# One signal per group, part or half; VectorE's row sum in a PSUM bank; row numbers in eight compare-and-multiply passes

## The reference, cut to what matters

```
# block 1 (cut): projection, 4-tap convolution, SiLU, chunked scan, gate, RMS norm, projection
zxbcdt = u @ W_in;  z, xBC, dt = split(zxbcdt)
xBC = silu(conv_b + sum_i pad(xBC)[i:i+s] * conv_w[i]);  x, B, C = split(xBC)
y = ssd(x * dt, -exp(A_log) * dt, B, C) + x * D
x1 = layernorm(u + rms(y * silu(z)) * norm_scale @ W_out)
# block 2: product-key retrieval, 8 heads, 8 rows each
h   = silu(x1 @ W_up.T + b_up) @ W_down.T + b_down
q   = h @ W_q.T                                    # two halves, 8 heads, 64 wide
sim = q . keys                                     # 64 keys in each half
scores, idx = top_k(sim, 8)                        # per half and head
all_scores  = sx[:, None] + sy[None, :]            # 64 pairs
all_indices = ix[:, None] * 64 + iy[None, :]
sc, pk  = top_k(all_scores, 8)
indices = take(all_indices, pk)                    # 64 row numbers per token
z   = silu((h . down_embed[indices]) * softmax(sc))
out = layernorm(x1 + sum_k z[k] * up_embed[indices[k]])
```

## Time and profile before

| | us |
|---|---|
| median of the runs (lowest, highest) | 3226.48 (3216.73, 3239.93) |
| the profiled execution, its own time | 3229.48 |
| its span, first to last instruction | 3227.5 |
| busy: TensorE, VectorE, ScalarE, GpSimd | 2906.3, 2840.0, 1672.4, 2251.4 |
| granted TensorE clock, mean | 0.959 |
| a gather, median from issue to landing | 4.7 |

### The profile page before, as it was taken

How to read it: one execution, slowest core, us unless ns; L and a number is a source line. 1 busy time by engine, 2 the same in 40 slices (tenths; PEclk the granted TensorE clock), 3 DMA queues, 4 the chain that set the end, 5 groups by cost and what they waited for, 6 DMA issues and landing times.

```text
span 3227.5 us, 50404 instructions
## 1 busy us (share of the span) xinstructions
PE 2906.3 (90%) x13856; PEld 1939.0 (60%) x13856; DVE 2840.0 (88%) x10664; ACT 1672.4 (52%) x4833; POOL 2251.4 (70%) x2056
## 2 busy tenths in 40 slices
PE   8899999999998999999998999999999999999864
PEld 8665566665556666556666655666665566665441
DVE  0579999899999999999999999999999999999986
ACT  0546554555555555555555565555555554555521
POOL 0047777777777777777777777777777777777776
PEclk9999999999999999999999999999999999999976
DMA  5258888888888888888888888888888888888887
GB/s 189 111 176 276 272 267 275 283 271 276 273 262 270 287 276 273 275 278 257 284 287 274 269 278 277 266 284 282 274 273 273 274 265 283 281 271 273 270 287 252
DMA packets 189354, 857.11 MB, mean 266 GB/s; under 512 B 36176, under 2 KB 39376, under 8 KB 188048
## 3 DMA queue, kind: packets, MB, share of 16 engines
q0 software_dynamic: 163840, 805.44, 76.2%
q1 hardware_dynamic: 19104, 34.87, 3.2%
q10 hardware_dynamic: 6128, 13.60, 1.1%
HBM read 845.38 MB, written 8.39 MB: 265 GB/s over the span
## 4 chain that ended last, share of the span: by engine, by line
DVE 41%; PE 29%; issue 10%; DMA 10%; ACT 7%; POOL 2%; DVEq 0%; POOLq 0%; ACTq 0%; SPq 0%
DVE acc L1053 11%; DVE ring L1034 10%; DMA ring<-embed,idx 9%; PE bank L457 9%; PE bank L416 7%; PE bank L307 4%; DVE xc L866 3%; PE bank L445 3%; POOL ring L262 2%; DVE i L953 2%; PE bank L290 2%; DVE v L946 1%; ACT L587 1%; ACT L676 1%; DVE zp L1040 1%
## 5 line engine op out<-in xcount | busy, mean ns | idle before, releaser
L262 POOL DMA_INDIRECT ring<-embed,idx x2048 | 2250.1, 1099 | 961.5 <-issue 494.6
L1034 DVE SCALAR_TENSOR_TENSOR ring<-ring,hcur 128x256 f32<-128x256 f32 x2048 | 831.2, 421 | 145.7 <-DMA ring<-embed,idx 141.0
L1053 DVE SCALAR_TENSOR_TENSOR acc<-ring,coef,acc 128x512 f32<-128x512 f32 x1248 | 935.3, 749 | 11.1 <-ACT coef L587 10.9
L457 PE MATMUL bank<-ring,diag_c 128*128 128x512 f32 x1536 | 812.9, 652 | 136.4 <-ACT diag_c L583 136.4
L583 ACT ACTIVATE diag_c<-cst,zp 128x128 f32<-128x128 f32 x768 | 278.6, 399 | 909.4 <-DVE zp L1040 877.7
L457 PEld LDWEIGHTS bank<-ring,diag_c 128*128 128x128 f32 x1536 | 289.8, 205 | 451.1 <-ACT diag_c L583 256.4
L416 PEld LDWEIGHTS bank<-zs,w_up 128*128 128x128 f32 x4096 | 470.8, 192 | 51.3 <-issue 31.2
L416 PE MATMUL bank<-zs,w_up 128*128 128x128 f32 x4096 | 476.4, 276 | 0.8 <-ACT zs L685 0.8
L307 PEld LDWEIGHTS bank<-ut,w_in 128*128 128x128 f32 x2560 | 293.6, 193 | 15.4 <-issue 15.4
L307 PE MATMUL bank<-ut,w_in 128*128 128x128 f32 x2560 | 293.9, 277 | 0.5 <-issue 0.5
L587 ACT ACTIVATE coef<-zp 128x3 f32<-128x3 f32 (+3 forms) x576 | 113.7, 197 | 333.9 <-DVE zp L1040 333.5
(11 more groups left out here) (132 smaller groups left out, 3544.8 us busy)
## 6 DMA issues: line engine op xcount, KB each, us to landing
ring<-embed,idx POOLq DMA_INDIRECT x2048, 4.7
ring<-uT SPq DMA_DIRECT2D x4, 2048.0 KB, 10.1
ut<-uT SPq DMA_DIRECT2D x32, 256.0 KB, 6.6
zs<-u SPq DMA_DIRECT2D x32, 256.0 KB, 5.7
out<-acc SPq DMA_DIRECT2D x32, 256.0 KB, 5.5
w_in<-W_in ACTq DMA_DIRECT2D x1, 4608.0 KB, 21.1
w_up<-W_upT ACTq DMA_DIRECT2D x1, 4096.0 KB, 19.1
w_out<-W_out ACTq DMA_DIRECT2D x1, 2048.0 KB, 9.5
```

What stands on the lines that cost most here:

```text
L262: pool.indirect_dma_start(out=ring[:, k % RING, :], out_offset=None, in_=embed, in_offset=bass.IndirectOffsetOnAxis(ap=idx[:, half, k:k + ...
L457: pe.matmul(bank[SUM][:, :], diag_c[:, n % DIAGS, :], ring[:, k % RING, DP:ROW], start=(n == 0), stop=(n == len(PE_ROWS) - 1)).then_inc(ro ...
L1034: dve.scalar_tensor_tensor(out=ring[:, k % RING, 0:DP], in0=ring[:, k % RING, 0:DP], scalar=1.0, in1=hcur[:, :], op0=ALU.mult, op1=ALU.mul ...
L1053: dve.scalar_tensor_tensor(out=total, in0=ring[:, k % RING, DP:ROW], scalar=coef[:, k:k + 1], in1=x1[:, :] if n == 0 else total, op0=ALU.m ...
```

## The change

It does six things.

1. `running`, the sum of the D rows, lies in PSUM bank 3. The first `weigh` of a tile reads `x1` and writes `running`, the next 38 read and write it, the last writes `total` in SBUF. The wait for `o_ok` moves from the first to the last.
2. The other stages share six banks instead of seven, so most of them move, with other waits. The third and the fourth step sum wait for the first and the second gate; `turn_x` begins after the first exponential; `z_proj` waits for the last convolution input; the up projections for `new_state`'s halves.
3. `row_pe` is signalled once per group, after its last P row; the gathers and ScalarE's buffers wait for the group. `DIAGS` is 4.
4. One signal per part of the convolution, per quarter of `up_silu`, per group of dots, for both halves of `y_off` and of `y_diag`.
5. Row numbers: mask and shift into one tensor `place`; then eight passes of 128 elements, each `(place == n) * i1[n]`, written with a stride of eight into `hot`; one reduction of 1024 elements.
6. The fence increments go, on VectorE, GpSimd and SyncE.

```diff
-DIAGS = 3
+DIAGS = 4
+PE_GRPS = [g for g in range(NGRP) if "P" in GROUPS[g]]
+NPG = len(PE_GRPS)
+def signal_of(k):
+    return PE_GRPS.index(max(g for g in PE_GRPS if FIRST[g] <= k)) + 1
...
-        hot = xdt[:, BANK:DI].rearrange("p (k c) -> p k c", k=PICKS)
+        hot = xdt[:, :].rearrange("p (g k a) -> p g k a", g=NG, a=TOP)
...
-        Z_BANKS, SEG_BANKS, XT_BANKS, MISC, YOFF_BANKS = (0, 2), (4, 1, 3, 0), (1, 3), 2, (4, 0)
-        Y_BANKS, ST_BANKS, YT_BANKS, OP, XBC_BANKS = (6, 7), (1, 3), (2, 4), 0, (6, 7, 1)
-        X1T, UP_BANKS, DOWN, HT, SIM_BANKS, SUM = 3, (2, 4, 0, 6), 7, 1, (6, 7), 5
+        Z_BANKS, SEG_BANKS, XT_BANKS, MISC, YOFF_BANKS = (0, 2), (4, 1, 0, 2), (4, 1), 0, (2, 0)
+        Y_BANKS, ST_BANKS, YT_BANKS, OP, XBC_BANKS = (6, 7), (4, 1), (2, 0), 6, (7, 2, 0)
+        X1T, UP_BANKS, DOWN, HT, SIM_BANKS, SUM = 6, (4, 1, 7, 2), 6, 6, (7, 6), 5
+        running = bank[3]
...
             def gathers(t, half, first):
                 pool.wait_ge(idx_ok, t + 1)
-                pool.sem_inc(pool_fence, 1)
...
-                            pool.wait_ge(row_pe, len(PE_ROWS) * of + PE_ROWS.index(j) + 1)
+                            pool.wait_ge(row_pe, NPG * of + signal_of(j))
...
-                        pool.sem_inc(pool_fence, 1)
...
             def step_sums(i, b):
-                if b == 0:
-                    pe.wait_ge(tap_ok, KC * (i + 1))
-                if b == 3:
-                    pe.wait_ge(z_ok, 2 * i + 1)
+                if b >= 2:
+                    pe.wait_ge(z_ok, 2 * i + b - 1)
...
-                    pe.matmul(bank[SUM][:, :], diag_c[:, n % DIAGS, :], ring[:, k % RING, DP:ROW],
-                              start=(n == 0), stop=(n == len(PE_ROWS) - 1)).then_inc(row_pe, 1)
+                    m = pe.matmul(bank[SUM][:, :], diag_c[:, n % DIAGS, :], ring[:, k % RING, DP:ROW],
+                                  start=(n == 0), stop=(n == len(PE_ROWS) - 1))
+                if rows_of(g, "P"):
+                    m.then_inc(row_pe, 1)
...
             def places(i):
                 dve.wait_ge(top2_ok, 4 * i + 2)
-                dve.tensor_scalar(bk[:, :], pk_v, TOP - 1, None, ALU.bitwise_and).then_inc(top2_ok, 1)
+                dve.tensor_scalar(place[:, 1, :, :], pk[:, :, :], TOP - 1, None, ALU.bitwise_and).then_inc(top2_ok, 1)
...
+                for n in range(TOP):
+                    dve.scalar_tensor_tensor(out=hot[:, :, :, n], in0=place[:, :, :, :].rearrange("p b n k -> p (b n) k"),
+                                             scalar=float(n), in1=i1[:, :, n:n + 1].to_broadcast([P, NG, TOP]),
+                                             op0=ALU.is_equal, op1=ALU.mult).then_inc(pick_ok, 1)
 
             def numbers(i):
+                dve.wait_ge(pick_ok, TOP * (i + 1))
+                dve.tensor_reduce(ixy[:, :, :], hot.rearrange("p (b n) k a -> p b (n k) a", b=2), AX.X, ALU.add).then_inc(ixy_ok, 1)
...
                 n = DVE_ROWS.index(k)
                 if n == 0:
                     dve.wait_ge(saved_ok, t + 1)
-                    if not first:
-                        dve.wait_ge(o_ok, t)
-                else:
+                if n > 0 or not first:
                     dve.wait_ge(row_used, len(DVE_ROWS) * t + n)
-                dve.scalar_tensor_tensor(out=total, in0=ring[:, k % RING, DP:ROW], scalar=coef[:, k:k + 1],
-                                         in1=x1[:, :] if n == 0 else total,
+                if n == len(DVE_ROWS) - 1 and not first:
+                    dve.wait_ge(o_ok, t)
+                dve.scalar_tensor_tensor(out=total if n == len(DVE_ROWS) - 1 else running[:, :],
+                                         in0=ring[:, k % RING, DP:ROW], scalar=coef[:, k:k + 1],
+                                         in1=x1[:, :] if n == 0 else running[:, :],
                                          op0=ALU.mult, op1=ALU.add).then_inc(row_used, 1)
```

More of the change, by code:

```diff
@@ L120, in build @@
         v2 = sb("v2", [P, EH, TOP])
-        pk = sb("pk", [P, EH, TOP], U32)
-        bk = sb("bk", [P, PICKS], U32)
-        ixy = sb("ixy", [P, 2, PICKS])
+        place = sb("place", [P, 2, EH, TOP], U32)
+        pk = place[:, 0, :, :]
         idx = sb("idx", [P, 2, PICKS], U32)
@@ L303, in xbc_proj @@
                         pe.wait_ge(y_ok, 2 * i)
-                        pe.wait_ge(st_ok, 2 * i - 1)
+                if part == 1 and not first:
+                    pe.wait_ge(yT_ok, 2 * i)
                 for c in range(4 * part, min(4 * part + 4, KC)):
@@ L350, in y_off @@
                 for b in range(2):
-                    pe.matmul(bank[YOFF_BANKS[b]][:, :], xc[:, KX + 1, :], state[:, b * BANK:(b + 1) * BANK],
-                              start=True, stop=True).then_inc(yoff_mm, 1)
+                    if b == 1:
+                        pe.wait_ge(dec_ok, 4 * i + 4)
+                    m = pe.matmul(bank[YOFF_BANKS[b]][:, :], xc[:, KX + 1, :], state[:, b * BANK:(b + 1) * BANK],
+                                  start=True, stop=True)
+                m.then_inc(yoff_mm, 1)
             def y_diag(i, first, b):
@@ L411, in up_proj @@
                     pe.wait_ge(x1T_ok, i + 1)
-                if b == 3 and ahead:
-                    pe.wait_ge(tap_ok, KC * (i + 1) + 4)
+                if b < 2:
+                    pe.wait_ge(st_ok, 2 * i + b + 1)
+                elif ahead:
+                    pe.wait_ge(tap_ok, PARTS * (i + 1) + b - 1)
                 for c in range(4 * b, 4 * b + 4):
@@ L434, in turn_h @@
                 pe.wait_ge(h_ok, i + 1)
-                if ahead:
-                    pe.wait_ge(tap_ok, KC * (i + 2))
                 for c in range(KP):
@@ L857, in time_steps, with convolve @@
                                          op0=ALU.mult, op1=ALU.mult).then_inc(cur_ok, 1)
-            def convolve(i, j, lo, hi):
-                for c in range(lo, hi):
-                    if j == 0:
-                        dve.wait_ge(tap_ok, KC * i + c + 1)
-                    else:
-                        dve.wait_ge(conv_ok, KC * (3 * i + j - 1) + c + 1)
-                    dve.scalar_tensor_tensor(out=xc[:, c, :], in0=raw[:, c, j:j + P], scalar=taps[:, c, j:j + 1],
-                                             in1=xc[:, c, :], op0=ALU.mult, op1=ALU.add).then_inc(conv_ok, 1)
+            def convolve(i, j, part):
+                if j == 0:
+                    dve.wait_ge(tap_ok, PARTS * i + part + 1)
+                else:
+                    dve.wait_ge(conv_ok, PARTS * (3 * i + j - 1) + part + 1)
+                for c in range(4 * part, min(4 * part + 4, KC)):
+                    m = dve.scalar_tensor_tensor(out=xc[:, c, :], in0=raw[:, c, j:j + P], scalar=taps[:, c, j:j + 1],
+                                                 in1=xc[:, c, :], op0=ALU.mult, op1=ALU.add)
+                m.then_inc(conv_ok, 1)
             def scaled_x(i):
@@ L992, in places @@
                 dve.wait_ge(top2_ok, 4 * i + 3)
[L993 to L999 removed]
+                dve.tensor_scalar(pk[:, :, :], pk[:, :, :], 3, None, ALU.logical_shift_right).then_inc(top2_ok, 1)
@@ L1029, in uses, with dot @@
                 return len(range(k % RING, PICKS, RING))
-            def dot(t, k):
+            def dot(t, k, last):
                 dve.wait_ge(row_in[k % RING], 16 * (uses(k) * t + k // RING + 1))
-                dve.scalar_tensor_tensor(out=ring[:, k % RING, 0:DP], in0=ring[:, k % RING, 0:DP], scalar=1.0,
-                                         in1=hcur[:, :], op0=ALU.mult, op1=ALU.mult,
-                                         accum_out=zp[:, k:k + 1]).then_inc(dot_ok, 1)
+                m = dve.scalar_tensor_tensor(out=ring[:, k % RING, 0:DP], in0=ring[:, k % RING, 0:DP], scalar=1.0,
+                                             in1=hcur[:, :], op0=ALU.mult, op1=ALU.mult,
+                                             accum_out=zp[:, k:k + 1])
+                if last:
+                    m.then_inc(dot_ok, 1)
             def times_prob(t, g):
-                dve.wait_ge(dot_ok, PICKS * t + FIRST[g + 1])
+                dve.wait_ge(dot_ok, NGRP * t + g + 1)
                 dve.tensor_tensor(zp[:, FIRST[g]:FIRST[g + 1]], zp[:, FIRST[g]:FIRST[g + 1]],
@@ L1074, in group @@
                     if n < len(mine):
-                        dot(t, mine[n])
+                        dot(t, mine[n], n == len(mine) - 1)
                     if n < len(late):
@@ L1184, in _ @@
             for j in range(TAPS - 1):
-                convolve(0, j, 0, KC)
+                for part in range(PARTS):
+                    convolve(0, j, part)
             dve.wait_ge(w_out_in, 16)
```

99 lines of the change are left out of this document (38 added, 61 removed).

## The result

The kernel after takes 3075.8 us (median of four runs, 3069.4 to 3081.0) against 3225.1 us for the kernel before beside it: ratio 0.9524, 95% interval 0.9498 to 0.955. The rival "All of it comes", 3079 us, is the case that came. The profiled execution has a span of 3070.2 us and a mean granted clock of 0.979 (before 0.959).

What follows compares the result with a forecast made beforehand. Bound: a loop through GpSimd's gathers, VectorE and TensorE, 94.8 us a tile. Terms -2.6 and -0.3 gave 91.9, taken as 92.3 beside floors 90.5 and 91.3; -2.5 us x 32 = -80 us: 3148 us, range 3080 to 3225.

Steps and rivals of the forecast that it cites:

- All of it comes: Rival for the whole kernel: relief 4.6 us, release hidden by the diagonal buffer, `weigh` cheaper; 3079 us, chance 0.12.
- the reserve behind the late release: On GpSimd behind gather 61: waits of gather 4 and the like (62, 0, 5) take up 0.7 us a tile.
- GpSimd is held by two-input instructions of VectorE: Gathers wait for VectorE's running instruction with two SBUF inputs to end; `weigh`s hold 5.2 us a tile.
- Relief 4.1 us in the loop: Row sum in PSUM: of 5.2 us of holding a tile, 4.1 lie between gathers 61 and 40 and go.
- Cost of a PSUM write: 0: VectorE's `weigh`s writing PSUM: no added cost, with bounds of +3.6 and -2.4 us a tile.
- Both rivals on a dearer `weigh`: VectorE's PSUM `weigh`: costly, at +0.14 us each 3271 us, chance 0.10; or +65 ns each, 3175 us, chance 0.14.
- The release, +2.2 us at gather 61: One signal per group: gather 61 waits for row 51, not row 48, adding 2.2 us a tile to the loop.
- Fences: nothing on GpSimd, 0.2 us on VectorE: Fence increments removed: no gain on GpSimd; on VectorE 0.05 us at five places, 0.2 us a tile.
- Banks: -0.3 us: New bank map: `turn_x` may begin earlier but step sums hold it; -0.3 us a tile in the loop.
- Numbers: -0.4 us: New row-number passes on VectorE, before gather 0's index: 0.4 us a tile saved.
- The floors, 90.5 and 91.3, and a loss of 0.4 to 0.8 where they meet: VectorE alone needs 90.5 us a tile, TensorE 91.3; with the loop's 91.9 they meet with loss, so 92.3.
- What would show it: Signs: gather mean about 1020 ns, `weigh` 0.75 us, row waits about 1.5 us, `h` waits below 2, DMA share 0.86.

Runs made afterwards that it cites:

- experiment 1: Kernel after with VectorE's running sum back in SBUF, all else as after: 3198.3 us, ratio 0.9917 to the kernel before.
- experiment 3: Kernel before with three more matmuls into `turn_h`'s own bank ahead of TensorE's wait for `h`: 3217.1 us, ratio 0.9953.
- experiment 2: Kernel after with old row numbers, fences, a signal per row, three diagonal buffers: sum in PSUM 3090.3 us, 0.957; sum in SBUF 3210.4 us, 0.9946.
- signals per row: Kernel after with `row_pe` signalled for every P row again, four diagonal buffers kept: 3062.1 us, ratio 0.9478 to the kernel before.
- experiment 4: Kernel after with `row_pe` for every P row: 3062.1 us, 0.9478; with only ScalarE's wait per row, gathers waiting for their group's last row: 3068.4 us, 0.9495.

## Why the prediction was wrong

The direction, the mechanism and the size of its main term were right; the sum was 69 us short. Three steps failed: the fences, which it put at nothing on GpSimd; the reserve behind the late release, which it sized too small; and the floors with the loss between them. Step by step:

*GpSimd is held by two-input instructions of VectorE.* Right, and shown by experiment 1 alone: 5.2 us of holding a tile, gone with one tensor's place. The rule that the prediction drew on (the Trainium skill, page SBUF — State Buffer, section Who interferes with whom) held on 20.6 gathers a tile that now run through a `weigh` unheld.

*Relief 4.1 us in the loop.* Right in size: the row sum in PSUM takes 3.9 us off the period in experiment 1 and 3.7 in experiment 2, while the gathers' durations fall by 5.3 and 4.8 us. That the quarter which doesn't count is the stretch between gathers 40 and 61 isn't shown: the prediction closed the loop through gather 40, `h` and TensorE, and experiment 3 speaks against `h` as its link. All edits together took 6.5 us out of the gathers: 5.2 by `weigh`, and 1.3 by the 2048-wide product and the convolution (holds 1.8 and 0.6 us before, 0.8 and 0.2 after). Those 1.3 us are luck of the new phases: a gather now slips in ahead of the product, and the next one meets its second half. With signals per row the two are 0.3 and 0.4.

*Cost of a PSUM write: 0.* Right: 752 ns, 0.66 us a step. The page's extra 62 cycles for a PSUM source (the Trainium skill, page VectorE: DVE Perf Modes, section The TRN2 errata — SBUF-src ops pay a fixed extra latency per instruction) would have made 814 ns by an estimate; no form here shows them. Both rivals on a dearer `weigh` fell with it.

*The release, +2.2 us at gather 61, 0.7 taken up by the reserve.* A failed step, some 30 us of the error. The wait itself is right in kind: before gather 61 it is 2.7 us a tile where it was 0.2. Net it costs 14 to 20 us, 0.4 to 0.6 us a tile, not the 1.5 of the sum, 48 us, since gathers 0 and 4 wait otherwise (1.4 and 0.9 us, experiment 4). The reserve behind it was under-sized by about a us. (The row of TensorE's group 16 in the earlier trace rows ends at the edge of its view; over a longer one it has all 8 matmuls and 3.70 us, and the step of 0.86 us stands.)

*Fences: nothing on GpSimd, 0.2 us on VectorE.* The failed step that is largest by time: 6 us were forecast, none of them in the loop of the sum, and 44 measured. The prediction read the cost off a gather that had nothing to wait for the earlier trace rows. The rows to read were those of a gather that waits: in the kernel before, too, gather 56 begins 0.82 us behind the end of its row, at 1696.21.

```profile
1695.19 1.02 PE L457 MATMUL bank<-ring,diag_c 128*128 128x512 f32 x2
...
1697.03 0.94 POOL L262 DMA_INDIRECT ring<-embed,idx  x1 [3.18 <-PE bank L457]
```

VectorE's was 0.5 us, since it passes a fence eight times a tile, not five, at 0.06 us on average and 0.11 at the norms.

*Banks: -0.3 us.* Measured 17 us with the part signals, 0.5 us a tile. The forecast new wait is there (L327, 0.7 us a tile), and `turn_x`'s wait of the same size is gone; that it is covered by the reserve which the prediction named is argued, not tried.

*Numbers: -0.4 us.* Right on VectorE (0.5); in time 4 to 11 us, not clear of noise.

*The floors, 90.5 and 91.3, and a loss of 0.4 to 0.8 where they meet.* The third failed step. The kernel after runs at 90.0 us, under both. Without the loss of 0.4 to 0.8 the sum is 13 us nearer. A floor made as period less wait takes everything that is left for work, and it wasn't. TensorE's work shrank by 1.4 us a tile (87.4 to 86.0) though no edit took a matmul away; the scores' return to 3.60 us and the clock's, at its lower level for 0.9 us a tile instead of 4.8, are most likely the reason. VectorE's shrank by 1.8 us instead of 0.6: numbers 0.5, fences 0.5, `weigh`s 0.5, the softmax products 0.2.

The parts don't quite add: 120 to 125 us for PSUM, 44 for the fences, 4 to 11 for the numbers, -14 to -20 for the group signals, 17 for banks and part signals make 165 to 183, not 149. The fences' term depends most on the rest. Between experiment 2 with PSUM and the signals per row lie the fences, the numbers and a diagonal buffer, and only 28 us, so with signals per row the fences are worth some 20; that a fence ahead of gather 61 costs less where that gather isn't late would explain it, and was not tried by itself. How the 17 us of banks and part signals split was not tried.

"What would show it" held in the gathers' mean (998, not above 1020), the 0.75 us of `weigh`, the DMA's landing (4.6 us) and its share (0.85). Its rival "All of it comes" has the time, but not by its own terms: the release wasn't hidden, and no `weigh` got cheaper. The waits for rows and for `h` fell further than said, 0.9 and 0.3 us a tile for 1.5 and under 2.

## What to carry to other kernels

Where GpSimd issues gathers beside VectorE, put the accumulator of VectorE's two-input passes in a PSUM bank, even at the price of a bank for the other stages: here it cost VectorE nothing and was worth 120 us of 3226. Read the cost of an edit off a row in the state that binds: a fence, or a signal moved to the end of a group, is free where nobody waits and is paid for at the three gathers in sixty-four that do. And before a period less a wait is called a floor, ask what of the rest is itself a consequence of the wait, the clock above all.

## What the runs showed of the hardware

- A gather (indirect DMA, 128 rows) takes 0.94 us on GpSimd and 0.30 to the next. One that begins 0.15 us or more behind the start of a VectorE instruction with two SBUF inputs is held to its end (498 of 503 beside a `weigh`; mean 1099 ns for all gathers, 2.79 us behind a product of 2.29); one that begins up to 0.05 us ahead or 0.08 us behind isn't (45 of 45). With one of the inputs in PSUM it isn't either (998 ns).
- From the end of a TensorE row to the start of a gather that waits for it: 0.27 us, and 0.82 us with a semaphore increment between the wait and the gather.
- After an idle 2.92 us TensorE's granted clock is 0.72 over 5 us and 1.00 in the next; with the wait filled it stays at 1.00 there, and in the tile shown it is 0.50 over 5 us behind the next idle time, of 1.84 us.
- 128x512 on VectorE, one input and the output in PSUM: 752 ns; all in SBUF: 749.
